# First attention of a gated two-layer block: stacked gate features, waits per quarter, another order of ScalarE's queue

## The reference, cut to what matters

```python
emb = box_relational_embedding(boxes)            # sin and cos of 100*log|..| of box distances, 16 features
g = relu(einsum('bnmd,hd->bhnm', emb, Wg) + bg)   # a gate for each head, query and key
q, k, v = queries @ Wq.T + bq, keys @ Wk.T + bk, values @ Wv.T + bv    # 16 heads of 64
a = einsum('bhqd,bhkd->bhqk', q, k) / 8
mn = softmax(log(clip(g, 1e-6)) + a)
out = einsum('bhqk,bhkd->bqhd', mn, v).reshape(b, nq, 1024) @ Wo.T + bo
x = x + tanh(g_xattn) * out
```

## Time and profile before

| | |
|---|---|
| median of 3 runs | 1144.31 us (1140.92 to 1145.85) |
| profiled execution | 1143.62 us, its span 1141.6 us |
| granted TensorE clock, mean | 0.929 |
| busy: PE, DVE, ACT, POOL | 83%, 72%, 60%, 62% |
| first attention | to about 471 us |

### The profile page before, as it was taken

How to read it: one execution, slowest core, us unless ns; L and a number is a source line. 1 busy time by engine, 2 the same in 40 slices (tenths; PEclk the granted TensorE clock), 3 DMA queues, 4 the chain that set the end, 5 groups by cost and what they waited for, 6 DMA issues and landing times.

```text
span 1141.6 us, 32938 instructions
## 1 busy us (share of the span) xinstructions
PE 949.0 (83%) x12178; PEld 777.1 (68%) x12178; DVE 817.9 (72%) x1957; ACT 684.2 (60%) x1342; POOL 710.1 (62%) x811
## 2 busy tenths in 40 slices
PE   0448999999999985589876569982899999999995
PEld 0336777777777764455544458861899999999995
DVE  3997888788877876677877689956566666666663
ACT  2457888888888883066543468854354454545452
POOL 2988888875777653035453279965466666666662
PEclk9889999999999997689988789985899999999998
DMA  9277776787767656411000100003553225832251
GB/s 280 76 188 150 135 150 153 157 175 171 146 154 159 137 109 167 143 51 41 1 1 1 40 2 21 21 21 100 165 152 103 33 40 168 268 91 32 32 143 14
DMA packets 52117, 119.65 MB, mean 105 GB/s; under 512 B 7616, under 2 KB 30144, under 8 KB 51632
## 3 DMA queue, kind: packets, MB, share of 16 engines
q0 software_dynamic: 14144, 35.48, 21.6%
q1 hardware_dynamic: 35520, 80.71, 21.1%
q10 hardware_dynamic: 2352, 2.10, 0.6%
HBM read 212.54 MB, written 37.85 MB: 219 GB/s over the span
## 4 chain that ended last, share of the span: by engine, by line
PE 53%; DVE 14%; POOL 11%; ACT 9%; DMA 7%; issue 5%; SPq 0%; ACTq 0%; POOLq 0%; DVEq 0%
PE bank L2168 17%; PE bank L2182 8%; POOL PT L565 6%; PE bank L1827 5%; PE bank L1730 3%; PE bank L1929 3%; DVE nmx L1209 2%; PE bank L1968 2%; PE bank L1807 2%; ACT EX L1424 2%; PE bank L1941 2%; PE bank L1769 2%; ACT L1393 1%; PE bank L1762 1%; DMA gates<-in_g_ffn 1%
## 5 line engine op out<-in xcount | busy, mean ns | idle before, releaser
L1664 ACT ACTIVATE yg<-bank,bms 128x128 f32<-128x128 f32 x312 | 106.9, 363 | 113.2 <-PE bank L2168 103.3
L1327 DVE TENSOR_TENSOR hm<-hf,hm 128x256 f16<-128x256 f32 x156 | 66.7, 427 | 90.8 <-ACT hm L1671 87.0
L1322 DVE SCALAR_TENSOR_TENSOR hf<-bank,bms,yg 128x128 f32<-128x128 f32 x312 | 98.8, 347 | 32.1 <-ACT yg L1664 29.4
L2168 PE MATMUL bank<-xT,wm_even 128*128 128x128 f16 x1920 | 116.2, 221 | 1.9 <-DVE xT L1334 1.0
L709 POOL DMA_INDIRECT out_x<-ys,sidx x39 | 62.7, 1608 | 83.2 <-DVE ys L1341 83.2
L2168 PEld LDWEIGHTS bank<-xT,wm_even 128*128 128x128 f16 x1920 | 111.5, 99 | 3.5 <-DVE xT L1334 1.4
L2168 PE MATMUL bank<-xT,wm_odd 128*128 128x128 f16 x1824 | 109.9, 220 | 2.0 <-DMA wm_odd<-expert_weights 2.0
L2168 PEld LDWEIGHTS bank<-xT,wm_odd 128*128 128x128 f16 x1824 | 105.5, 99 | 3.1 <-issue 2.2
L1671 ACT ACTIVATE hm<-hf 128x256 f16<-128x256 f32 x156 | 64.7, 415 | 63.9 <-DVE hf L1322 62.8
L565 POOL TENSOR_TENSOR PT<-PT 128x512 f16<-128x512 f32 x64 | 72.3, 1157 | 41.7 <-ACT PT L1450 41.6
L551 POOL TENSOR_TENSOR q<-qt,q 128x512 f16<-128x512 f32 x64 | 79.9, 1276 | 1.0 <-ACT q L1437 0.9
(11 more groups left out here) (309 smaller groups left out, 2660.2 us busy)
## 6 DMA issues: line engine op xcount, KB each, us to landing
wm_even<-expert_weights SPq DMA_DIRECT2D x60, 1024.0 KB
wm_odd<-expert_weights SPq DMA_DIRECT2D x57, 1024.0 KB
expert_weights<-in_wcat POOLq DMA_DIRECT2D x16, 768.0 KB, 7.8
wsp<-expert_weights SPq DMA_DIRECT2D x16, 768.0 KB, 4.4
wsp<-in_wcat POOLq DMA_DIRECT2D x16, 768.0 KB, 10.6
expert_weights<-wsp SPq DMA_DIRECT2D x16, 768.0 KB, 3.3
Lst<-gate_tables SPq DMA_DIRECT2D x48, 68.0 KB, 5.8
gate_tables<-Lw SPq DMA_DIRECT2D x6, 512.0 KB, 4.6
```

Of the source, the lines that this page charges most:

```text
L1322: v.scalar_tensor_tensor(hf[:, (c // 2) % 2, c % 2, :], bank[c % 4][:, MT:2 * MT], bms[:, par, FC + c:FC + c + 1], yg[:, c % 4, :], ALU.ad ...
L1327: v.tensor_tensor(hm16[:, par, 1, c - 1:c + 1, :], hf[:, q % 2, :, :], hm16[:, par, 0, c - 1:c + 1, :], ALU.subtract).then_inc(m_hl, 1)
L1664: s.activation(yg[:, c % 4, :], bank[c % 4][:, 0:MT], ACT.Gelu, bias=bms[:, par, c:c + 1]).then_inc(m_g, 1)
L2168: ins = t.matmul(bank[c % 4][:, w * MT:(w + 1) * MT], wm16[par][:, wp, col:col + P], xT16[:, par, xp * KD + kk, :], start=(n == 0), stop=( ...
```

## The change: what it does

- The features are put in groups of 32 partitions that hold 4 queries of the block (`QN`). After the sine, 12 DMAs per element (SyncE, `stack_high`, `stack_low`) copy them from SBUF to SBUF into `Fst`: for each of the four groups q, 96 partitions with the high features twice and the low ones once. `We16` has 96 rows and 64 columns (high, low, high). A gate group then has eight matmuls of 64 columns instead of six of 256; all three products of a pair are summed in one.
- `F16s` and `Fst` have one buffer each; ScalarE's high copy and GpSimd's low part wait for the stacks of the element before, TensorE's first gate group for those of its own (`s_fst`).
- SyncE's queue is written per element; the stacks stand ahead of the store and load of the expert halves, and the second table store comes one element earlier in the queue, ahead of the stacks of element 7.
- `pv` waits for each low quarter by itself. The wait for `s_opt` becomes one for `s_xu`.
- VectorE: the norm of b+3 stands ahead of the probabilities of b (it was the norm of b+2 at the head of the iteration); bn_stats comes an iteration later, between other work.
- ScalarE: the sine of b and its high copy come right behind the high probabilities of b-1, instead of behind the exponentials of the iteration before; take_o is ahead of the logarithm, both halves of the values behind it.
- The boxes' rows are spread over the partitions before the launch; two loads instead of four.

```diff
+QN = 4
+QR = 2 * QN * 4
+FR = 3 * QR
+STK = 16 * 3 * (NN // QN)
...
-        F16s = sb("F16s", [P, 2, 2, NJ * N], F16, l0)
+        F16s = sb("F16s", [P, 2, NJ * N], F16, l0)
+        Fst = sb("Fst", [P, NN // QN, NJ * N], F16, l0)
...
-            for xy in range(2):
-                for e in range(2):
-                    sp.dma_start((cm, rows)[e][64 * xy:64 * xy + 64, :], a["boxm"][xy, e, :].partition_broadcast(64)).then_inc(s_cw, 16)
+            for e in range(2):
+                sp.dma_start((cm, rows)[e][:, :], a["boxm"][e]).then_inc(s_cw, 16)
...
+            def stack_high(b):
+
+                sp.wait_ge(s_fhi, b + 1)
+                if b:
+                    sp.wait_ge(s_gf, 4 * b)
+                for q in range(NN // QN):
+                    for k in range(2):
+                        sp.dma_start(Fst[k * QR:k * QR + QR, q, :], F16s[q * QR:q * QR + QR, 0, :]).then_inc(s_fst, 16)
+
+            def stack_low(b):
+
+                sp.wait_ge(s_flo, b + 1)
+                for q in range(NN // QN):
+                    sp.dma_start(Fst[2 * QR:3 * QR, q, :], F16s[q * QR:q * QR + QR, 1, :]).then_inc(s_fst, 16)
+
             for par in range(2):
                 next_ctx(par, par)
+            stack_high(0)
             store_tables(0)
             for par in range(2):
                 load_tables(par)
+            stack_low(0)
             for par in range(2):
                 load_half(0, par, True)
-            for i in range(1, B // 2 - 1):
-                for par in range(2):
-                    next_ctx(i * 2 + par, par)
-                    if i * 2 + par == NJ:
-                        store_tables(1)
-                    load_tables(i * 2 + par)
-                    store_half(i - 1, par)
-                    load_half(i, par)
-            for par in range(2):
-                load_tables(B - 2 + par)
-                store_half(E - 2, par)
-                load_half(E - 1, par)
-
+            for b in range(2, B):
+                par = b % 2
+                if b < B - 2:
+                    next_ctx(b, par)
+                load_tables(b)
+                stack_high(b - 1)
+                stack_low(b - 1)
+                store_half(b // 2 - 1, par)
+                load_half(b // 2, par)
+                if b == NJ - 1:
+                    store_tables(1)
+
+            stack_high(B - 1)
+            stack_low(B - 1)
             store_half(E - 1, 0)
...
             def feature_low(n, par):
                 gp.wait_ge(s_fhi, n + 1)
-                nc.gpsimd.tensor_tensor(F16s[:, par, 1, :], fs, F16s[:, par, 0, :], ALU.subtract).then_inc(s_flo, 1)
+                if n:
+                    gp.wait_ge(s_fst, STK * n)
+                nc.gpsimd.tensor_tensor(F16s[:, 1, :], fs, F16s[:, 0, :], ALU.subtract).then_inc(s_flo, 1)
...
             def iteration(b, par, has_c, has_q, has_x, first=False):
-                if has_x:
+                if not has_c:
                     norm(b + 2, b + 2)
                 row_max(b, (0, 1))
                 if has_q:
                     take_qk(b + 1, (0, 1))
+                if b > 1:
+                    v.bn_stats(bst[:, b - 2, :], X[:, b - 2, :])
                 row_max(b, (2, 3))
...
                     feature_distance(b + 2, par)
+                if b + 3 < B:
+                    norm(b + 3, b + 3)
                 probs(b, not has_c)
-                if has_c:
-                    v.bn_stats(bst[:, bass.ds(b - 1, 1), :]...)
...
-                if first > 1:
-                    ac.wait_ge(s_gf, 4 * n - 4)
-                s.activation(F16s[:, par, 0, :], fs, ACT.Copy).then_inc(s_fhi, 1)
+                if n:
+                    ac.wait_ge(s_fst, STK * n)
+                s.activation(F16s[:, 0, :], fs, ACT.Copy).then_inc(s_fhi, 1)
...
             def iteration(b, par, c, has_x, has_q=True):
                 if c:
                     probs_high(b - 1, c == 1)
+                    feature_sine(b, par, c)
                 if has_x:
                     ctx_high(b + 2, par, False)
                 if has_q:
                     qk_high(b + 1, 1 - par, range(4))
                     feature_abs(b + 1, 1 - par)
-                    feature_log(b + 1, 1 - par)
-                    v_high(b + 1, 1 - par, (0,))
                 if c:
                     take_o(b - 1, c == 1)
                 if has_q:
-                    v_high(b + 1, 1 - par, (1,))
+                    feature_log(b + 1, 1 - par)
+                    v_high(b + 1, 1 - par, (0, 1))
...
                 exps(b, par, c == 0)
-                if has_q:
-                    feature_sine(b + 1, 1 - par, min(c + 1, 2))
...
                 if g == 0:
-                    pe.wait_ge(s_flo, b + 1)
+                    pe.wait_ge(s_fst, STK * (b + 1))
                     pe.wait_ge(s_tl[par], (b - par) * 24 + 48)
...
-                    for n, (wp, fp) in enumerate(PAIRS):
-                        ins = t.matmul(bk[:, jj * 256:(jj + 1) * 256], F16s[:, par, fp, j * N:(j + 1) * N], We16[:, wp, :], start=False,
-                                       stop=(n == 2), skip_group_check=True)
+                    part = bk[:, jj * 256:(jj + 1) * 256].rearrange("p (h q i) -> p q h i", h=H, q=NN // QN)
+                    for q in range(NN // QN):
+                        ins = t.matmul(part[:, q, :, :], Fst[0:FR, q, j * N:(j + 1) * N], We16[0:FR, :], start=False, stop=True,
+                                       skip_group_check=True)
...
             def pv(c, par, first):
-                pe.wait_ge(s_pl, 4 * c + 4)
                 pe.wait_ge(s_vl, 2 * c + 2)
                 for f in range(4):
+                    pe.wait_ge(s_pl, 4 * c + f + 1)
...
-                            pe.wait_ge(s_opt, c)
+                            pe.wait_ge(s_xu, c)
```

40 lines of the change are left out of this document (21 added, 19 removed).

## The result

The changed kernel takes 1219.33 us (median; 1216.89 to 1222.23) against 1144.55 for the kernel before on the same chip: 1.066 times as long (95% interval 1.0625 to 1.0694). Slower was forecast, at 1154; it is 65 us more than that. The profiled execution has a span of 1218.0 us against 1141.6, 76.4 more.

| stretch | before | after | more |
|---|---|---|---|
| start to H of iteration 1 | 93.98 | 98.73 | +4.8 |
| to H of iteration 2 | 24.95 | 25.94 | +1.0 |
| 12 of the next 13 periods | 23.63 each | 27.30 each | +44.0 |
| the one with the second table store | 23.67 | 37.51 | +13.8 |
| the last period | 24.59 | 38.46 | +13.9 |

What follows compares the result with a forecast made beforehand. TensorE had little room (22.57 of 23.64 us busy); after the change ScalarE's 23.47 us loop would set the period. Terms -2.9 - 1.3 + 6.2 + 6.0 + 2.0 = +10.0 us gave 1154 us, forecast 1150 to 1162 (45%).

Steps and rivals of the forecast that it cites:

- The stacking DMAs in the steady state: SyncE's twelve stack transfers per iteration, 0.42 us per issue, 5.04 us; landing before the first gate group needs them, costing 0.
- E+23.0 by the median: Stack's landing at median 5.8 us, counted from an iteration's first exponentials (E); needed at E+23.9, so no cost.
- Rival (c): The stack lands 1.5 us late at TensorE's gate in every iteration; 1173 us, 10% chance.
- The closest place, the turned output: ScalarE's output copies: output turned by about 9.2 us after high probabilities start, wanted at 8.9 and 9.4; wait 0 to 0.2.
- ScalarE's 23.47: ScalarE's loop per iteration without a wait on another engine, 6.51 plus 16.96 us; said to set the period.
- One-time costs: Second table store +6.2 us, FFN weights loaded behind the last stack +6.0, accumulating load beside them +2, start 0.15 later.
- were all of them on the path: Upper bound for the later start, from the norm and SyncE's first eight stacking issues put ahead: 3.4 us.
- Steady -2.9: Gain over 13 attention iterations at a period of 23.47 us, the last one 0.69 less: 304.42 us instead of 307.27.
- rival d: Weight loads pace TensorE's 64-column gate matmuls; a group stays at 1.09 us, total 1156 us; 5% chance.
- Rival (a): TensorE's chain is the bound and its 1.6 us cut counts whole, 14 times: -22.4, 1136 us; 14% chance.
- rival (b): ScalarE's loop as forecast, but single costs at their low ends: +4.3, about 1148 us; 26% chance.
- a group of 1.17 us: Gate group by the skill page's 107 ns weight load: TensorE's path 24.0 us, the sum some 6 us larger.

Runs made afterwards that it cites:

- e3: Changed kernel with GpSimd's copy of an expert half put behind the context's low half instead of ahead of v's; 1202.5 us, 1.050.
- e4: Changed kernel with the high features stacked once, 8 transfers instead of 12, leaving out the low-weights times high-features product; 1181.0 us, 1.033.
- e2: Kernel before with all edits but the stacking, SyncE's new order and the box loads; 1149.9 us, 1.007.
- e15: Changed kernel with the logarithm and first high half of v ahead of the turned output again; 1203.8 us, 1.054.
- e1: Changed kernel with the sine and its high copy back behind the exponentials; 1180.3 us (1163 to 1193), 1.033.
- e5: Changed kernel with ScalarE's whole old order: e1 plus logarithm and first high half of v ahead of the turned output; 1165.0 us, 1.022.
- e7: e1 with 32 overwritten matmuls added on TensorE between the first gate group and the second scores; 1161.8 us, 1.019.
- e12: Changed kernel with three SyncE queue places changed: first table store, second table store, FFN weight loads; 1194.7 us, 1.047.
- e6: e5 with three SyncE queue places changed: first table store, second table store, FFN weight loads; 1143.5 us, 1.004.
- e18: e6 with the sine's high copy behind the high probabilities and the norm behind the products again; 1142.5 us, 0.998.
- e13: e6 with VectorE's eight distances moved from ahead of the products to behind xn's low half; 1149.6 us, 1.007.
- e10: e6 with VectorE's eight distances moved from ahead of the products to between v's two evictions; 1190.4 us, 1.041.

## Why the prediction was wrong

The direction was right, the size wasn't: the profiled execution took 76.4 us more where the sum had 10. The stacks, the turned output and the one-time costs were too small, and one cause, the clock, was missing.

**The stacking DMAs in the steady state (0 forecast): the main failure.** Two terms failed. Twelve issues at 0.42 us, from the Lst loads, were 8.3 us: 0.63 from one to the next, and one of 1.42. And "E+23.0 by the median" took the light stretch of DMA for granted, which the trace before has only to E+18 (a share of 0.42 and 0.50 from E+12, then 0.88 to E+23.6); the last stack issue of the sum lay at its very end. The median landing is even shorter (2.0 us), but it is the last one that counts, and it took 7.36 because GpSimd's half copy had gone out at 341.34, 0.7 us ahead of it. Moving that copy (e3) ends nearly all of the waits, and so does dropping four transfers (e4), with which the last one goes out ahead of it. Rival (c) had this mechanism at 1.5 us and 10%; TensorE waited 3.4 in the period shown.

**The closest place, the turned output (0 to 0.2).** 0.67 us in e2 and 1.83 in the changed kernel. ScalarE's 23.47 was right as a sum of its work. But before, the logarithm stood in that wait, and with its table load now behind, the wait comes on top: 0.6 us a period in e2. In the changed kernel the 1.83 us don't all come back: e15 is 15 us shorter, but in its profiled execution only 5.5 of 11.0 us are in the loop's other periods. Between e1 and e5 lie 15 us too, but e1's runs spread by twice that.

**The clock (not in the prediction).** I took 1.00 from the earlier trace rows as given. Behind idle stretches of 2.05 us (e1, e3) and 3.39 us the level was at times the lower one (1.2 GHz), with scores at 1.46 instead of 0.84 us (e1) and a 48-matmul projection at 4.7 instead of 2.85 (e3). e7 shows the cause: fill the stretch, and it goes. Why the same gap costs at one time and not at another isn't shown.

**One-time costs.** SyncE's queue order cost 25 us (e12) where I had 14.4 (6.2, 6.0, 2 and the 0.2 of the start). The start was +4.8 with eight issues (5.06 us) ahead of the tables; the bound "were all of them on the path" of 3.4 was the better choice, with the true issue price. The store's iteration was 10.2 over its neighbours (6.2), and the last +13.9 (8). All three have the 0.63 us per issue in them. The last also has weights that took 15.8 us to land, not 11.3 (I had +2); GpSimd's accumulating load went out beside them at 505.69, as forecast, but no run takes it away alone.

**Steady -2.9.** Without stacks the reordering gives +0.6 a period (e2) where the sum had -0.2. The steps that held are the gate group's 0.65, ScalarE's 2.87 idle and no effect of the weight loads (rival d). Rival (a), TensorE as the bound, is false: e6 takes 1.7 us off its busy time and the period stays. The sums come out as written but for two that the forecast doesn't use: rival (b) is nearer 1149, and a group of 1.17 us gives by the prediction's own terms a path of 23.8 and 5 us more, not 24.0 and 6.

Not settled: why e6 has the period of the kernel before over another chain, why the store's iteration is 6.6 us shorter in e15, what shortens e18's period, and whether e1's order would gain with the stack's issues shared out to another queue. That wasn't tried.

## What to carry to other kernels

Price a transfer's issue from rows with the same number and form of transfers in a row, and its landing from what other engines issue next to it, not from the median. Before an engine's work is cut, follow the cycle that closes the period and see whether the work is on it: here four shorter groups were worth nothing, since no gate group was on the cycle. When a change makes no difference, read the chain again: the kernel before and e6 have the same period over different chains. An order that opens a gap on TensorE can cost more than the gap; look at the granted clock of the stretch behind it.

## What the runs showed of the hardware that I hadn't expected

- Twelve SBUF-to-SBUF transfers of 64 KB, issued in a row by SyncE: 0.59 us each and 0.04 between, against 0.42 for Lst's. They land in 1.9, 2.0 and 7.8 us (least, median, most).
- The same idle gap of 2.05 us on TensorE was followed by a clock of 1.00 and by 0.50 in one execution (e1), which spread its runs over 30 us. 32 small matmuls in the gap brought that down to 6.
- A VectorE instruction of 0.33 us took 2.80 while GpSimd worked (e13), and eight of them 6.28 instead of 2.14 (e10).
